# Memory stage: the sums of squares begin with minus one, and ScalarE clears the room below zero

## The reference, cut to what matters

```
x = (x - jnp.max(x, -1, keepdims=True)) / 2.0
xs = jnp.flip(jnp.sort(x, -1), -1)
rho = jnp.arange(1, x.shape[-1] + 1)
mean = jnp.cumsum(xs, -1) / rho
meansq = jnp.cumsum(xs * xs, -1) / rho
ss = rho * (meansq - jnp.square(mean))
tau = mean - jnp.sqrt(jnp.clip((1.0 - ss) / rho, 0.0, None))
support = jnp.sum(tau <= xs, -1, keepdims=True)
tau_star = jnp.take_along_axis(tau, support - 1, -1)
return jnp.square(jnp.clip(x - tau_star, 0.0, None))
```

## Time and profile before

| | us |
|---|---|
| median of 3 runs | 1814.58 |
| lowest and highest | 1812.86, 1815.31 |
| the profiled execution, its own time | 1812.72 |
| its span in the trace | 1810.9 |
| memory stage in it, first `add_gap` to last `bound` | 478.9 to 1263.8 |

### The profile page before, as it was taken

The page is one execution under the profiler, slowest core; times in us unless marked ns, Lnnn a source line. Parts: engine busy times, 40 slices in busy tenths (PEclk is TensorE's granted clock), DMA queues, the critical chain, the costliest instruction groups (busy, mean ns, idle before and its releaser), DMA issues. The chain is left out here.

```text
span 1810.9 us, 25659 instructions
## 1 busy us (share of the span) xinstructions
PE 1557.9 (86%) x7346; PEld 1091.4 (60%) x7346; DVE 1362.2 (75%) x3568; ACT 1151.7 (64%) x2769; POOL 751.9 (42%) x2049
## 2 busy tenths in 40 slices
PE   5889999998577879877997789877779999999987
PEld 2546657466455668766786678666645556555554
DVE  6666757572489899999999999999644566767646
ACT  3243342413278888889989998999447565665630
POOL 3414224150356666677767776677310101001000
PEclk9699999998877899989998999899899999999989
DMA  5000000000000000030000000000000000000000
GB/s 231 1 1 1 1 1 1 1 1 0 1 1 1 1 1 1 1 112 1 1 1 1 1 1 1 1 1 1 1 1 1 1 1 1 1 13 1 13 1 24
DMA packets 6716, 19.21 MB, mean 11 GB/s; under 512 B 1072, under 2 KB 4144, under 8 KB 5296
## 3 DMA queue, kind: packets, MB, share of 16 engines
q1 hardware_dynamic: 6576, 17.58, 2.6%
HBM read 15.48 MB, written 2.10 MB: 10 GB/s over the span
## 5 line engine op out<-in xcount | busy, mean ns | idle before, releaser
L1316 DVE BATCH_NORM_STATS2 r_moments<-mem_arena 128x6 f32<-128x512 f32 x576 | 382.7, 683 | 4.2 <-ACT mem_arena L1638 4.1
L1638 ACT ACTIVATE mem_arena<-mem_arena,r_shift 128x256 f32<-128x256 f32 x792 | 351.3, 512 | 38.7 <-POOL r_shift L1533 38.7
L1706 PE MATMUL r_bank<-arena,r_wT 128*128 128x256 f32 x1024 | 243.8, 399 | 10.1 <-ACT mem_arena L1638 8.1
L1706 PEld LDWEIGHTS r_bank<-arena,r_wT 128*128 128x128 f32 x1024 | 203.1, 201 | 46.4 <-issue 17.2
L1723 PE MATMUL r_bank<-ident,mem_arena 128*128 128x128 f32 x576 | 107.1, 322 | 93.1 <-DVE mem_arena L1332 80.7
L1280 DVE MAX8 r_top<-r_bank 128x8 f32<-128x256 f32 x384 | 145.4, 417 | 26.5 <-PE r_bank L1706 24.3
L1723 PEld LDWEIGHTS r_bank<-ident,mem_arena 128*128 128x128 f32 x576 | 79.2, 165 | 131.0 <-DVE mem_arena L1332 65.7
L2293 ACT ACTIVATE arena<-arena,e_NM 128x512 f32<-128x512 f32 (+3 forms) x256 | 134.3, 558 | 29.2 <-DVE e_NM L1981 29.2
L1706 PE MATMUL r_bank<-arena,r_xnT 128*128 128x256 f32 x512 | 122.6, 401 | 18.2 <-ACT mem_arena L1638 17.0
L1981 DVE CUSTOM_DVE_ANT_0 arena<-e_banks,ffn_then_moe 128x512 f32<-128x512 f32 (+3 forms) x256 | 110.1, 485 | 28.9 <-PE e_banks L2498 28.5
L1316 DVE BATCH_NORM_STATS2 r_moments<-r_u 128x6 f32<-128x512 f32 x192 | 129.2, 684 | 2.5 <-ACT r_u L1638 2.4
(11 more groups left out here) (324 smaller groups left out, 3315.9 us busy)
## 6 DMA issues: line engine op xcount, KB each, us to landing
ffn_then_moe<-in_w SPq DMA_DIRECT2D x3, 1024.0 KB, 14.4
out_x<-X SPq DMA_DIRECT2D x4, 512.0 KB, 2.9
X<-in_x SPq DMA_DIRECT2D x1, 1536.0 KB, 11.4
w_in<-in_w_in SPq DMA_DIRECT2D x1, 1156.0 KB, 6.2
mem_arena<-in_wq SPq DMA_DIRECT2D x1, 1024.0 KB, 16.6
mem_arena<-in_wo SPq DMA_DIRECT2D x1, 1024.0 KB, 20.9
ffn_then_moe<-in_gate SPq DMA_DIRECT2D x1, 1024.0 KB, 7.3
ffn_then_moe<-in_up SPq DMA_DIRECT2D x1, 1024.0 KB, 9.3
```

What stands on the lines that cost most here:

```text
L1316: last = dve.bn_stats(moments[:, a.lane, 2 * p:2 * p + 2, :].rearrange("p two c -> p (two c)"), u[a.lane][:, 2 * p:2 * p + 2, :].rearrange ...
L1638: last = act.activation(u[a.lane][:, h, :], u[a.lane][:, h, :] if k else scores[:, h, :], ACT.Relu, bias=shift[:, a.lane, h:h + 1])
L1706: last = pe.matmul(scores[:, h, :], lhs, (G1 if a.first else G2)[:, h, i, :], start=i == 0, stop=i == 1)
```

## The change

Column 0 of the squares is the square of the largest minus itself, always 0. It is now set once to -1 for all lanes, and `square` writes the other seven columns. The running sums of squares then are ss' - 1, and times -1/k they hold the 1/k that `add_room` added: `add_gap` takes over the name `add_room`, and the old one (L1503), at the head of POOL's slot, goes. DVE's `clear` (L1288) goes too. ACT waits for the room and clears it with a Relu in place, drains, and takes the root as before.

```diff
@@ square, POOL
-                y = fold[0][:, a.lane, 0:NHM, PAD:]
+                y = fold[0][:, a.lane, 0:NHM, PAD + 1:]
...
-                pool.tensor_tensor(fold[0][:, a.lane, NHM:, PAD:], y, y, ALU.mult).then_inc(squared, 1)
+                pool.tensor_tensor(fold[0][:, a.lane, NHM:, PAD + 1:], y, y, ALU.mult).then_inc(squared, 1)
@@ before POOL's loop
+            pool.memset(fold[0][:, :, NHM:, PAD:PAD + 1], -1.0)
@@ add_gap and add_room, POOL
-                pool.tensor_tensor(room[:, a.lane], room[:, a.lane], back[:, a.lane], ALU.add).then_inc(gap_ready, 1)
...
-                pool.wait_ge(gap_ready, of_unit(a))
-                pool.tensor_tensor(room[:, a.lane], room[:, a.lane], inv_k[:], ALU.add).then_inc(room_ready, 1)
+                pool.wait_ge(msq_ready, of_unit(a))
+                pool.tensor_tensor(room[:, a.lane], room[:, a.lane], back[:, a.lane], ALU.add).then_inc(room_ready, 1)
@@ POOL's loop
-                add_room(Unit(n - 3))
...
-                add_gap(Unit(n - 2))
+                add_room(Unit(n - 2))
@@ DVE's clear, and its call
-                dve.wait_ge(room_ready, of_unit(a))
-                dve.tensor_scalar(room[:, a.lane], room[:, a.lane], 0.0, None, ALU.max).then_inc(clear_ready, 1)
...
-                clear(Unit(n - 4))
@@ bound_root, ACT
-                act.wait_ge(clear_ready, of_unit(a))
+                act.wait_ge(room_ready, of_unit(a))
+                act.activation(room[:, a.lane], room[:, a.lane], ACT.Relu)
+                act.drain()
                 act.activation(room[:, a.lane], room[:, a.lane], ACT.Sqrt).then_inc(troot_ready, 1)
```

More of the change, by code:

```diff
@@ L1209, in memory_block @@
             "stats_ready", "rstd_ready", "xn_ready", "xnT_in_psum", "xnT_ready"))
-        scores_done, top_ready, centred, squared, sum2, sum4, sum8, mean_ready, msq_ready, gap_ready, room_ready = (
+        scores_done, top_ready, centred, squared, sum2, sum4, sum8, mean_ready, msq_ready, room_ready = (
             sem(n) for n in ("scores_done", "top_ready", "centred", "squared", "sum2", "sum4", "sum8", "mean_ready",
-                             "msq_ready", "gap_ready", "room_ready"))
-        clear_ready, troot_ready, back_ready, bound_ready, start_ready = (sem(n) for n in (
-            "clear_ready", "troot_ready", "back_ready", "bound_ready", "start_ready"))
+                             "msq_ready", "room_ready"))
+        troot_ready, back_ready, bound_ready, start_ready = (sem(n) for n in (
+            "troot_ready", "back_ready", "bound_ready", "start_ready"))
         clipped, dve_clipped, moments_ready, inv_ready, s2_ready, root_ready, shift_ready = (
@@ L1282, in largest @@
                         last.then_inc(top_ready, 1)
-            def clear(a):
-                if not a.live:
-                    return
-                dve.wait_ge(room_ready, of_unit(a))
-                dve.tensor_scalar(room[:, a.lane], room[:, a.lane], 0.0, None, ALU.max).then_inc(clear_ready, 1)
             def bound(a):
@@ L1491, in mean_square, with add_room @@
                 pool.tensor_tensor(back[:, a.lane], mean8[:, a.lane], mean8[:, a.lane], ALU.mult).then_inc(msq_ready, 1)
-            def add_gap(a):
+            def add_room(a):
                 if not a.live:
@@ L1496, in add_gap @@
                 pool.wait_ge(msq_ready, of_unit(a))
-                pool.tensor_tensor(room[:, a.lane], room[:, a.lane], back[:, a.lane], ALU.add).then_inc(gap_ready, 1)
-            def add_room(a):
-                if not a.live:
-                    return
-                pool.wait_ge(gap_ready, of_unit(a))
-                pool.tensor_tensor(room[:, a.lane], room[:, a.lane], inv_k[:], ALU.add).then_inc(room_ready, 1)
+                pool.tensor_tensor(room[:, a.lane], room[:, a.lane], back[:, a.lane], ALU.add).then_inc(room_ready, 1)
             def step_back(a):
```

## The result

The changed kernel takes 1826.89 us, the median of four runs (1826.46 to 1828.53), beside 1814.49 for the kernel before (1812.86 to 1815.31): a ratio of 1.0071, 95% interval 1.0059 to 1.0083, or +12.4 us. It is slower, as forecast, but by more than three times the +3.7 forecast, and above the range's end of 1823.0. A second set of runs on another chip gives a smaller loss (experiment 1: +7.6 us).

What follows compares the result with a forecast made beforehand. Two nearly equal loops, POOL-DVE and ACT's way, were taken to bound the slot. Terms 1.7 + 0.6 + 1.7 + 0.6 - 0.2 - 0.7 + 0.5 - 0.1 - 0.4 = +3.7 us gave 1818.3 us, range 1812 to 1823.

Steps and rivals of the forecast that it cites:

- Two tight loops: Steady slot: POOL-DVE loop sets 15.66 us, ACT's way has 0.09 us spare and takes over once the Relu is added.
- Rival 1: Only the POOL-DVE loop is tight, ACT takes up its 0.32 us in idle time: 13 us faster, 1801.6; chance 0.09.
- Rival 2: ACT's lateness is half absorbed, only tile slots pay: +0.3 us, 1814.9, nothing to measure; chance 0.15.
- Relu and drain: On ACT ahead of the root: Relu 0.25 us and drain 0.07 us, with 0.02 and 0.14 kept open for the drain.
- Rival 3: Drain costs 0.14 us as POOL's, a table load between dependent instructions 1.28 us more: +7.5 us, 1822.1; chance 0.10.
- The steady slot: 13 slots without output or new tile go from 15.66 to 15.79 us through ACT's way: +1.7 us together.
- slots 19 and 28 to 31: With slot 18, six slots where DVE came late to `clear` and ACT had 0.03 us more spare: 6 x 0.10 = +0.6 us.
- Slots 23 and 35: Two tile slots without output work behind them, late through pass 0: 2 x 0.31 = +0.6 us.
- Output slots: Nine with a new tile: bound 0.19 us later each, +1.7 us; units 15, 27, 39 without one: -0.07 each, -0.2.
- Units 0 to 3: Unit 0 +0.94 us, table load now behind the Relu; units 1 and 2 gain 0.31 and 0.15; unit 3 loses 0.19.
- The clock: Early units' +1.0 us counted half, +0.5, since score blocks that start later meet less of the slow 1.2 GHz stretch.
- rival 4: Extra time moves score blocks into slow stretches, 2.6 us a block, two more blocks: 1823.5 us; chance 0.08.

Runs made afterwards that it cites:

- experiment 1: No edit: the kernel before and the changed kernel run again on a second chip; 1816.35 us before, 1823.9 us after, ratio 1.0042.
- experiment 2: Against the changed kernel, DVE clears as before and ACT has only the root, POOL's sums still beginning with minus one (POOL's half alone); 1812.85 us, ratio 0.9983.
- experiment 3: Against the changed kernel, the sum L1503 stays on POOL while ACT clears with Relu and drain (ACT's half alone); 1825.13 us, ratio 1.0051.
- experiment 7: Against experiment 2's kernel, ACT takes the root of pass 1 directly behind the bound's root; 1807.28 us, ratio 0.9968 to the kernel before.
- experiment 8: Against the kernel before, only ACT's root of pass 1 moved directly behind the bound's root; 1815.7 us, ratio 1.0008.
- experiment 5: Against the changed kernel, a root of one column at the head of ACT's list brings the table load there; 1824.08 us, ratio 1.0059 to the kernel before.
- experiment 6: Against the changed kernel, Relu and drain are done twice; 1841.13 us, ratio 1.0153 to the kernel before.
- experiment 4: Against the changed kernel, DVE's clip of pass 3, head 7, goes ahead of the bound; 1824.54 us, ratio 1.0054 to the kernel before.
- experiment 9: Against the changed kernel, ACT takes the root of pass 1 directly behind the bound's root; 1818.1 us, ratio 1.0018 to the kernel before.
- experiment 10: Against the changed kernel, one DVE moments instruction goes between the bound and the clip of head 7; 1820.59 us, ratio 1.0035 to the kernel before.

## Why the prediction was right in direction and wrong in size

The forecast is 8.7 us short of the first comparison and 3.9 short of the second. Two terms of the sum failed in both: the steady slots, through one duration on ACT's way, and the clock. They are marked below; on the first chip the clock is the larger.

- **Two tight loops, right.** The view that the POOL-DVE loop and ACT's way are both near to the limit, and that ACT's takes over, is borne out by experiments 2, 3, 7 and 8. By the prediction's own numbers ACT's way without the Relu would give 15.66 + 0.13 - 0.32 = 15.47 us; experiment 2's 15.60 has the collision on top. Rival 1 (ACT takes up its 0.32 us in its idle time) falls: the idle time before the clip grew from 0.17 to 0.33. Rival 2 (half absorbed) falls with the steady slots.
- **Relu and drain, right.** The drain costs 0.07 us, as taken, in 46 of 48 units; once it is 1.35 with the load in it, and once 0.36, with an idle time that is put down to issue. Rival 3 falls with it: neither POOL's 0.14 nor a load that holds ACT for longer than its own length is seen.
- **The steady slot, wrong: the first step that failed.** "The slot becomes 15.79": it is 15.91. The sum had every instruction on ACT's way at its duration in the trace before, L1533 at 0.20 us among them. That duration depends on what DVE does beside it. Counted from ACT's start on the shift of pass 2, the change moved POOL's L1533/L1521 from +3.77 to +3.97 and DVE's clip behind the bound from +3.99 to +3.92 (the bound is 0.08 earlier, forecast 0.07). So the shift, which ended 0.02 us before the clip, now starts 0.05 us inside it. Slot by slot, from POOL's start on pass 0 to the next, in the second pair of traces, the 13 slots of this kind grew by 3.1 us together, forecast 1.7, and slots 19 and 28 to 31 by 1.0, forecast 0.5: 1.9 us more in 18 slots. They do not share it evenly (slot 32 has +0.52, slots 20 and 34 +0.07), and I have not followed that further.
- **Slots 23 and 35, a little too small.** They grew by 0.42 and 0.41 us, forecast 0.31 each: 0.2 us together. The shift takes 0.35 us there too.
- **Output slots, right.** With a new tile +0.23 (forecast +0.19), without one -0.07 (forecast -0.07).
- **Units 0 to 3, right in unit 0 and wrong in what follows.** Unit 0's bound is 0.98 us late (forecast 0.94). That it counts at the end was wrong: the way from unit 0's bound to unit 1's is 0.7 us shorter in the first pair of traces and 1.0 in the second, and experiment 5 shows no gain from taking it away.
- **The clock, wrong: the second step that failed.** The steps had +1.0 us for the feed-forward units, halved for the clock. Units 4 to 12 grew by 1.8 to 3.7 us. Of this 1.7 is unit 5's block: 8.4 to 8.5 us in the five traces where DVE clears, 9.9 to 10.2 in the seven where ACT clears once. In experiment 6 it is 9.1, and unit 4's is 10.1. So rival 4 came true in part: one block in each of the seven traces, three in the first. Unit 34's block is also slow (8.8) in experiment 3's trace, so what was lost there in the first trace can come back. PE is idle for 0.46 us ahead of unit 5's block in the first five and for 0.61 to 0.88 in the seven; whether that is the cause was not tried, and it stays open.

Put together from unit 0's bound on, in the second pair of traces: -1.3 us for units 0 to 4, +1.8 for 4 to 12, -0.6 for 12 to 18 and +6.6 from there on (the forecast's terms there are 1.7 + 0.6 + 1.1 + 0.6 - 0.1 - 0.3 = 3.6), that is +6.5, and with unit 0's own 1.0 it is +7.5, beside 7.6 between the medians on that chip. (The spans of the two traces differ by 5.2 only: the stage began 1.1 us earlier, without unit 0's own, and what follows it was 1.2 shorter.) In the first pair there are, besides, 3.3 us of half clock in units 34 and 44, 1.9 more in units 4 to 12, and a stage that began later: the room without its 1/k, ahead of all that the change touches but `square`, was there at 479.20 before and at 481.78 after, 2.6 us later. Why the first chip's medians lie 12.4 us apart and the second's 7.6 is only partly told by this, since other executions have no trace.

With 0.12 us for the collision in each of the 19 slots from unit 18 on that have neither output nor new tile, the forecast would have been 3.7 + 2.3 = +6.0; with unit 5's 1.7 us it would have been +7.7, or 1822.3. That is near the second comparison's +7.6, and still 4.6 short of the first chip's 1826.9: what is missing there is in part the half clock in other blocks, which stood in rival 4 and not in the sum, and the later start of the stage, which stood nowhere.

## What to carry to other kernels

A duration read from a trace belongs to its neighbours too: before moving work by a tenth of a microsecond, look what the other engines run beside the instruction that ends the chain, and look for like rows with two durations (0.20 and 0.35 here), which name the collision that waits. Where two loops have nearly one length, an edit on either measures as nothing or as a loss and both together as a gain, so try them together before giving either up. Clear or clamp where the engine with spare time stands, not on the one whose way closes the slot: in the changed kernel one more 0.25 us instruction with a drain made each steady slot 0.31 us longer (experiment 6), since nothing hid it.

## What the runs showed of the hardware

- A POOL `tensor_tensor` of 128x8 that starts inside a DVE `tensor_scalar` of 128x256 ends 0.06 us behind it: 0.35 us for 0.20 in 34 of 48 units of the changed kernel, and in 23 of 48 with POOL's half alone. Beside DVE's moments (BATCH_NORM_STATS2) it keeps its 0.20.
- A drain of ACT between two dependent instructions costs 0.07 us; with a table load between them as well the gap is 1.35 us, 1.28 of it the load. The Trainium skill gives 1380 ns of drain on top of the load (ScalarE: Activation LUTs, What ACT_TABLE_LOAD costs); the next instruction starts 0.02 us behind the load here (482.12 + 1.28 to 483.42), so this trace does not agree.
- In the changed kernel one root, that of unit 39, starts 0.60 us behind its Relu instead of 0.31, in both executions, and so it does in experiments 3, 4, 9 and 10; in experiment 5, with one more instruction at the head of ACT's list, no unit does. In experiment 6 three instructions start late, in units 17, 20 and 46. So it goes with the program and not with the execution; the trace puts such idle time (0.34 us) down to issue, and the cause stays open.
- A block of scores that runs at full clock in one execution of a program can lose 1.7 us in another (units 34 and 44: 8.83 against 7.15), and the stage of one program can begin 2 us apart (480.5 and 482.7). Single traces of two kernels should not be subtracted without a second of each.
